# Sums of the scan's states on TensorE: accumulating fp32 transposes for steps 0 to 11, and no half sums on GpSimd

## What is computed

```
def step(h, inputs):
    dA_t, dBu_t, C_t = inputs
    h = h * dA_t + dBu_t
    y = jnp.einsum('bdn,bn->bd', h, C_t)
    return (h, y)
...
return y + u * D
...
y = y * jax.nn.silu(res)
out = y @ W_out + x
```

## Time and profile before

| | us |
|---|---|
| median of three runs | 954.75 |
| lowest and highest run | 954.55, 956.04 |
| span of the profiled execution, first to last instruction | 952.4 |
| scan of batch 0, from its first scan instruction | about 111 to 165 |
| scans of batches 1, 2 and 3 | 304.4 to 378.9, 518.9 to 593.3, 734.3 to 808.6 |
| TensorE busy | 851.5 (89%) |
| VectorE busy | 634.7 (67%) |
| ScalarE busy | 365.3 (38%) |
| GpSimd busy | 358.4 (38%) |

### The profile page before, as it was taken

One profiled execution on the slowest core, in us unless ns is written; L12 is line 12 of the kernel. 1 busy time (PEld: TensorE's weight loads), 2 busy tenths in 40 slices (PEclk: granted clock), 3 DMA queues, 4 the chain that ended last, 5 costly groups with the idle time before them and its releaser, 6 DMA issues.

```text
span 952.4 us, 12787 instructions
## 1 busy us (share of the span) xinstructions
PE 851.5 (89%) x4568; PEld 641.6 (67%) x4568; DVE 634.7 (67%) x1322; ACT 365.3 (38%) x788; POOL 358.4 (38%) x390
## 2 busy tenths in 40 slices
PE   6897677989999998889999998889999998679997
PEld 5675455754787886754787886753787887426886
DVE  6242599885447989885347989884446989754333
ACT  5111554426415443326415443326325443253110
POOL 4302396220044775220044775220044876000322
PEclk9998888999999999999999999999999999999999
DMA  7202310020036330320026330320024330300452
GB/s 223 106 8 81 138 51 0 1 102 14 1 100 207 113 116 1 111 82 33 1 96 209 114 117 0 111 83 33 1 67 153 107 123 6 111 2 1 142 156 77
DMA packets 26929, 76.12 MB, mean 80 GB/s; under 512 B 3436, under 2 KB 5420, under 8 KB 26228
## 3 DMA queue, kind: packets, MB, share of 16 engines
q1 hardware_dynamic: 26612, 75.26, 24.2%
q10 hardware_dynamic: 256, 0.07, 0.0%
HBM read 74.13 MB, written 1.11 MB: 79 GB/s over the span
## 4 chain that ended last, share of the span: by engine, by line
PE 54%; DVE 28%; issue 10%; ACT 5%; POOL 2%; DMA 1%; ACTq 1%; DVEq 0%; POOLq 0%; SPq 0%
PE B L801 27%; PE F L801 20%; DVE arena L1446 12%; PE B L1076 3%; DVE arena L1458 3%; DVE nmx L1518 2%; PE F L830 1%; DVE q_t L1579 1%; ACT big L768 1%; DVE arena L1279 1%; PE F L812 1%; POOL rs L472 1%; PE B L1157 1%; DMA room<-in_w_l 1%; DVE q_t L1584 1%
## 5 line engine op out<-in xcount | busy, mean ns | idle before, releaser
L801 PE MATMUL B<-spare,mw 128*128 128x256 f32 x880 | 208.6, 380 | 1.5 <-DMA mw<-in_w_moe 1.2
L801 PEld LDWEIGHTS B<-spare,mw 128*128 128x128 f32 x880 | 165.6, 190 | 26.8 <-DMA mw<-in_w_moe 2.5
L1446 DVE TENSOR_TENSOR_SCAN arena<-F,arena 128x512 f32<-128x512 f32 x128 | 148.7, 1206 | 1.6 <-ACT F L728 1.5
L492 POOL TENSOR_TENSOR arena<-du,arena 128x1024 f32<-128x1024 f32 x60 | 140.7, 2357 | 20.0 <-PE B L801 17.8
L583 POOL TENSOR_TENSOR spare<-q_t 128x256 f32<-128x256 f32 x112 | 80.7, 728 | 172.6 <-DVE q_t L1584 161.7
L728 ACT ACTIVATE F<-delta,a_neg 128x255 f32<-128x255 f32 x256 | 109.4, 467 | 57.7 <-DVE arena L1446 57.7
L801 PE MATMUL B<-mw,spare 128*128 128x256 f32 x448 | 114.3, 380 | 0.0
L790 ACT ACTIVATE q_t<-B 128x256 f32<-128x256 f32 x112 | 41.9, 380 | 159.7 <-PE B L801 156.6
L801 PEld LDWEIGHTS B<-mw,spare 128*128 128x128 f32 x448 | 84.6, 190 | 12.8 <-issue 1.0
L768 ACT ACTIVATE big<-B 128x512 f32<-128x512 f32 x128 | 69.4, 594 | 51.7 <-PE B L801 45.3
L1579 DVE SCALAR_TENSOR_TENSOR q_t<-q_t,B 128x256 f32<-128x256 f32 x112 | 46.6, 416 | 58.8 <-ACT q_t L790 58.6
(11 more groups left out here) (233 smaller groups left out, 1288.0 us busy)
## 6 DMA issues: line engine op xcount, KB each, us to landing
mw<-in_w_moe SPq DMA_DIRECT2D x112, 384.0 KB, 3.1
room<-in_w_f SPq DMA_DIRECT2D x4, 2544.0 KB, 9.0
arena<-b_out SPq DMA_DIRECT2D x32, 256.0 KB, 4.9
room<-in_w_l SPq DMA_DIRECT2D x4, 768.0 KB, 6.8
w_m<-in_w_m SPq DMA_DIRECT2D x1, 2112.0 KB
room<-in_w_l SPq DMA_DIRECT2D x4, 512.0 KB, 5.1
x_t<-in_x_t SPq DMA_DIRECT2D x4, 256.0 KB, 3.7
x_tok<-in_x_tok SPq DMA_DIRECT2D x4, 256.0 KB, 7.0
```

Of the source, the lines that this page charges most:

```text
L492: g.tensor_tensor(state(n).rearrange("p d (s t) -> p d s t", s=2), du[:, 2 * dp:2 * dp + 2, :].unsqueeze(2).to_broadcast([P, 2, 2, S]), b_ ...
L801: return t_.matmul(dst, lhsT, rhs, start=start, stop=stop, skip_group_check=True)
L1446: v.tensor_tensor_scan(h, F[i][:, :], h, 0.0, ALU.mult, ALU.add)\
```

## The change

The sums of steps 0 to 11 (NTURN is 12) become transposes that accumulate. The state of a step is cut in eight squares of 128 x 128; each is loaded as the stationary operand, and the identity is streamed past it with the transpose flag, so that the square arrives in PSUM turned over, with tokens on the partitions, and is added there. F[3] then holds the sum of all 512 channels for token tile 0 and K[2] that for token tile 1: each step writes both banks. In phase s13 ScalarE copies the two banks to SBUF (`xt`, `xb`) after the decay of step 14 and ahead of that of step 15; in phase s14 TensorE turns them back by eight transposes (`turn_back`), which start the banks anew in the old layout, and the states of steps 12 to 15 are added as before, now always with four products. `pair_sum` and its waits are gone. Step 0 now touches K[2], so the wait for x4_read moves from step 1 to step 0.

```
--- before.py
+++ after.py
@@ -34,6 +34,7 @@
 DT = DI // P
 NK = NS // 2
 NSTEP = 2 * NK
+NTURN = 12
 RING = 5
 HQ, HKV, HD1 = 32, 8, 8
 HG = HQ // HKV
@@ -347,10 +348,6 @@
 
             return K[2] if dp else F[3]
 
-        def in_halves(b, n):
-
-            return n % 2 == 1 and n < NSTEP - 1 and later(b)
-
         def c_on_pool(b, n):
 
             return n % 4 == 1 and not later(b)
@@ -495,13 +492,6 @@
                                 .to_broadcast([P, 2, 2, S]), ALU.mult)\
                     .then_inc(gf.step(f"dbu{n}"), 1)
 
-            def pair_sum(b, n):
-
-                pool.wait_ge(*df.at(f"hc{n}", b))
-                h = state(n)
-                g.tensor_tensor(h[:, :, 0:S], h[:, :, 0:S], h[:, :, S:2 * S], ALU.add)\
-                    .then_inc(gf.step(f"half{n}"), 1)
-
             def front(b, ph):
                 if ph in PAIRS:
                     n = 2 * PAIRS.index(ph) + 1
@@ -557,8 +547,6 @@
                     n = STEPS.index(ph)
                     if n + 2 < NSTEP:
                         scan_input(b, n + 2)
-                    if n >= 1 and in_halves(b, n - 1):
-                        pair_sum(b, n - 1)
                     if c_on_pool(b, n):
                         pool.wait_ge(*df.at(f"scan{n}_1", b))
                         pool.wait_ge(*af.at(f"cc{n}", b))
@@ -707,6 +695,10 @@
                     scan_decay(b, 0)
                 if ph in STEPS[:-1]:
                     scan_decay(b, STEPS.index(ph) + 1)
+                if ph in STEPS and STEPS.index(ph) == NTURN + 1:
+                    act.wait_ge(*pf.at(f"y{NTURN - 1}", b))
+                    for t, dst in enumerate((xt, xb)):
+                        copy(dst[:, :, :].rearrange("p a n -> p (a n)"), y_bank(t)[:, :], af, f"yt{t}")
                 if ph in STEPS and c_on_pool(b, STEPS.index(ph) + 1):
                     n = STEPS.index(ph) + 1
                     if n >= 5:
@@ -870,18 +862,41 @@
                 k, dp = divmod(n, 2)
                 if n == 0:
                     pe.wait_ge(*af.at("delta0", b))
-                if n == 1 and later(b):
+                if n == 0 and later(b):
                     pe.wait_ge(*db.at("x4_read", b - 1))
                 if n < NSTEP - 1:
-                    pe.wait_ge(*(gf.at(f"half{n}", b) if in_halves(b, n) else (gf if c_on_pool(b, n) else df).at(f"hc{n}", b)))
-                parts = 1 if in_halves(b, n) else 2
+                    pe.wait_ge(*(gf if c_on_pool(b, n) else df).at(f"hc{n}", b))
+                if n < NTURN:
+                    for t in range(TT):
+                        for i in range(2):
+                            for s in range(2):
+                                c, d = s * S + t * P, (2 * dp + i) * P
+                                last = t_.matmul(y_bank(t)[:, d:d + P], state(n)[:, i, c:c + P], ident[:, :],
+                                                 start=(n == 0 and i == 0 and s == 0),
+                                                 stop=(n >= NTURN - 2 and s == 1),
+                                                 is_transpose=True, skip_group_check=True)
+                    last.then_inc(pf.step(f"y{n}"), 1)
+                    return
                 for i in range(2):
                     if n == NSTEP - 1:
                         pe.wait_ge(*df.at(f"hc{n}_{i}", b))
-                    for s in range(parts):
+                    for s in range(2):
                         last = mm(y_bank(dp)[:, i * S:i * S + S], ident[:, :], state(n)[:, i, s * S:s * S + S],
-                                  k == 0 and i == 0 and s == 0, k == NK - 1 and s == parts - 1)
+                                  False, k == NK - 1 and s == 1)
                 last.then_inc(pf.step(f"y{n}"), 1)
+
+            def turn_back(b):
+
+                for t in range(TT):
+                    pe.wait_ge(*af.at(f"yt{t}", b))
+                for dp in range(2):
+                    for i in range(2):
+                        for t, src in enumerate((xt, xb)):
+                            d = (2 * dp + i) * P
+                            t_.matmul(y_bank(dp)[:, i * S + t * P:i * S + t * P + P],
+                                      src[:, :, :].rearrange("p a n -> p (a n)")[:, d:d + P], ident[:, :],
+                                      start=(i == 0 and t == 0), stop=False, is_transpose=True,
+                                      skip_group_check=True)
 
             def scan_out(b, i):
 
@@ -1054,6 +1069,8 @@
                     n = STEPS.index(ph)
                     if n % 2 == 0:
                         spread_c(b, n)
+                    if n == NTURN + 2:
+                        turn_back(b)
                     if n >= 2:
                         sum_states(b, n - 2)
                     if n == NSTEP - 1:
```

## The result

The changed kernel takes 959.96 us (median of 20 runs, 952.91 to 962.3), the kernel before 954.68 in the same comparison (20 runs, 952.04 to 958.6). The changed kernel spreads over 9.4 us from run to run and the kernel before over 6.6, far more than the three runs of before had shown; the experiments explain this in part. Executions at a clearly lower clock throughout (here one of the kernel before at 1271.73 us and one of a later kernel at 969.01) are left out of every ratio. The profiled execution has a span of 959.8 us where before had 952.4, so 7.4 us are to be found in the two traces.

A forecast was written before the change was run, and what follows sets the result against it. VectorE was taken to set batch 0's pace, with TensorE late only mid-scan in later batches. Terms -5.1 + 0.3 + 1.5 + 1.7 + 3.0 = +1.4 on the median of 954.75 gave 956.2 us, range 951.4 to 960.8.

The forecast's parts named there:

- Part 4: Scan ends: TensorE's clock falls when idle ahead of dense work; +1.7 us in batch 0, +3.0 over the later batches.
- Prices: TensorE's sums: 0.109 us per transpose, 0.22 at half clock; a transposed state 0.87 us against 1.73 for a whole one.
- rival (c): Transposed sums: each transpose of a fresh state costs its whole 0.27 us; total near 972 us, chance 0.04.
- Part 1: Middle of each later scan: shorter sums of steps 2 and 4 gain 1.7 us, -5.1 us over three scans.
- Rival (d): Middle of later scans: VectorE's waits stay because another engine holds things up; 961.3 us, or 956.6 without clock losses; chance 0.09.
- One sign to look for: Later scans: VectorE's waits of 0.82, 0.83 and 0.92 us all gone or down to a tenth.
- Part 2: Ends of later scans: copies, turn_back and four queued sums cost 0.1 us each at full clock, +0.3 for three batches.
- Part 3: End of batch 0's scan: the copies delay turn_back and four sums without cover, +1.5 us.
- Rival (b): Ends of all scans: transposes do not hold the clock, so it stays low through turn_back and after; 961.8 us, chance 0.13.
- Rival (a): Ends of later scans: the clock holds there; 953.1 us, or 951.4 if in batch 0 too; chance 0.24.

The follow-up runs named there:

- the filler: The changed kernel with TensorE's idle time ahead of turn_back filled by unread products, six in batch 0, four in each later batch: 949.66 us, ratio 0.994.

## Why the prediction was right or wrong

It held in its range (951.4 to 960.8) and in its direction, and was short in size: it gave 956.2 us, 1.4 slower than before, and the kernel is 4.3 slower by the ratio. The measured 959.96 lies above the forecast's own 954.7 to 957.7. It had called a difference within 0.2% the likeliest (0.43), and slower by a measurable amount came out (0.38). The mechanism was the forecast one; the term that was too small is Part 4. Point by point:

- **Prices.** Right. The transposed sums run at 0.109 us a transpose, 0.22 at half clock; rival (c) is out.
- **Part 1**, the middle: -5.1 forecast, -5.1 measured (1.71, 1.69, 1.66), and it came where TensorE was late, as forecast. Rival (d) is out. One sign to look for was stated wrongly, though the sum had it right: the wait of 0.83 stays (0.85 in each later scan), since VectorE gets there earlier by as much as TensorE; only the waits of 0.82 and 0.92 go.
- **Part 2**, the queue at the later ends: 0.3 forecast. With the clock held by the filler the ends take 8.31 in place of 8.27, so 0.1 for three. Right in kind, and small as forecast.
- **Part 3**, the queue at batch 0's end: +1.5 forecast, +1.3 measured with the filler. Right.
- **Part 4**, the clock in batch 0: the mechanism is right, the size is not. I took the low clock for the first 3.4 us of dense work (+1.7). It lasted 5.4 us, from 160.13 to 165.5, as it had already fallen when that work began, and cost 2.8.
- **Part 4**, the clock at the later ends: forecast in two of three at 1.5, in all +3.0; measured in three of three at 1.7, in all +5.0. This is the term furthest off. I took it for a matter of chance at two in three; it fell in eleven of twelve such ends that were traced, so chance remains, at higher odds. The stretch I compared it with the earlier trace rows kept the clock once in two cases with 1.54 and 1.53 us of work in 3.4; the last 3.4 us ahead of `turn_back` in batch 1 hold 1.35. Why it fell almost every time here is not shown.
- With Part 4 at its measured size the sum is -5.1 + 0.1 + 1.3 + 2.8 + 5.0 = +4.1, the +4.1 of the scans in the two traces, against 4.3 (3.0 to 5.6) in the ratio. That the second agrees so closely is partly luck: the ratio also holds the executions of either kernel in which the clock fell more or less often than in the trace.
- **Rival (b)** gave +7.1 us, about as far above the measured +4.3 as the forecast lies below it, but for a reason that is not the case: transposes as such do not let the clock fall. With the idle time ahead of them filled, by products or by transposes, it holds.
- **Rival (a)**, the clock holds at the later ends, is in no trace. It gave 953.1; the two short executions of twenty, 952.91 and 953.18, are where it may have happened.
- **Not in the sum at all**: the 3.9 us after the last scan. They are over half of the 7.4 us between the two traces. The kernel before probably has them in some executions (filler there gained it 2.2 us), and three runs did not show the spread. Whether the change makes that stretch more frequent was not settled: the traces of the changed kernel have it and the one of before has not, but so has the trace of the kernel before without half sums, and five kernels with transposed sums have not.

## What to carry to other kernels

When work is taken from an engine whose clock follows its activity, list the idle gaps that this leaves and what dense work stands behind each; here the low clock behind such gaps cost 7.8 us, more than the 5.1 gained, and four idle products in a later scan and six in batch 0's bought that back. Place a step that others must wait for (a copy and its use) where the queues behind it still have slack: two steps earlier made the same edit 0.7% faster than the kernel before, where it had been 0.45% slower. And before trusting a difference of some us between two profiles, compare the stretches that the edit does not touch.

## What the runs showed of the hardware

- fp32 transposes of 128x128 that accumulate in PSUM run at 0.109 us each at 2.4 GHz and 0.22 at 1.2 GHz. A stretch of 2.8 us of nothing else kept the granted clock at 1.00, and behind one spread of C and 2.8 us of them (152.7 to 155.5) it rose from 0.50 to 0.99.
- In the changed kernel TensorE was 13.45 of 17 us busy at 1.2 GHz, and the clock did not rise in them; in the kernel before, in the same attention phase, it was 5.48 of 10 us busy at 2.4 GHz (828 to 838) before the clock fell for 3.4 us. In the changed kernel, products in the 2.2 us of idle time ahead of the stretch were enough to keep the 3.9 us. A product takes longer at the lower clock, so busy shares at the two levels do not compare as amounts of work.

```profile
828.00:838.00 10.00, 5.48 (x20) 1.20 (x20) 9.96 (x11) 0.37 (x1) 0.00 (x0) 1.00 0.00 0
```
